# An audio tower kernel: the 3x3 convolution as four products side by side, and a new order of the pipeline behind it

## The reference, cut to what matters

```
h = signature(x) @ W.T + b                      # 64 x 63 tokens, 128 features
a = layernorm(h)
q = batchnorm(a @ Wq + bq); k = softmax(a @ Wk + bk); v = batchnorm(a @ Wv + bv)
lam_c = einsum('bukt,buvt->bkv', k, v);   Yc = einsum('bhkt,bkv->bhvt', q, lam_c)
lam_p = relu(conv3x3(v, Wpos));           Yp = einsum('bhkt,bkvt->bhvt', q, lam_p)
h = h + (Yc + Yp) @ Wout + bout
c = layernorm(h)
h = h + top1_expert(c; gate_w, w1, w2, w3) + gelu(c @ sw1.T) @ sw2.T
```

## Time and profile before

| what | value |
|---|---|
| median of 3 runs | 637.65 us |
| the profiled execution, its time | 638.09 us |
| its span, first to last instruction | 636.1 us |
| busy: PE / DVE / POOL / ACT | 587.9 / 501.1 / 304.1 / 278.7 us |
| granted TensorE clock, mean | 0.975 of full speed |

### The profile page before, as it was taken

How to read it: one execution, slowest core, us unless ns; L and a number is a source line. 1 busy time by engine, 2 the same in 40 slices (tenths; PEclk the granted TensorE clock), 3 DMA queues, 4 the chain that set the end, 5 groups by cost and what they waited for, 6 DMA issues and landing times. The chain is left out here.

```text
span 636.1 us, 13527 instructions
## 1 busy us (share of the span) xinstructions
PE 587.9 (92%) x3737; PEld 469.5 (74%) x3737; DVE 501.1 (79%) x1407; ACT 278.7 (44%) x693; POOL 304.1 (48%) x307
## 2 busy tenths in 40 slices
PE   2789999999999999999895999999999899999993
PEld 0467888888888888888663677777777678888882
DVE  6968889999999988887764788988788677777772
ACT  3332233333333332331224667676767745555541
POOL 3924334555544443320033468887767553333332
PEclk9798999999999999999998899999999999999997
DMA  8402455566665544555655545554441322222210
GB/s 285 45 1 86 153 180 179 187 196 201 202 188 184 163 145 154 163 168 169 154 125 168 126 102 135 126 130 103 112 106 46 93 77 80 74 59 76 60 32 1
DMA packets 127171, 80.02 MB, mean 126 GB/s; under 512 B 66548, under 2 KB 121485, under 8 KB 127126
## 3 DMA queue, kind: packets, MB, share of 16 engines
q1 hardware_dynamic: 122642, 72.89, 40.7%
q0 software_dynamic: 3296, 6.27, 3.1%
q10 hardware_dynamic: 1188, 0.30, 0.2%
HBM read 30.64 MB, written 49.33 MB: 126 GB/s over the span
## 5 line engine op out<-in xcount | busy, mean ns | idle before, releaser
L1251 DVE SCALAR_TENSOR_TENSOR P<-PS,QN 128x512 f32<-128x512 f32 x128 | 79.5, 683 | 26.3 <-PE PS L1430 25.7
L553 DVE SCALAR_TENSOR_TENSOR Z<-PS,Vt,Z 126x128 f32<-126x128 f32 x224 | 78.6, 351 | 8.6 <-PE PS L681 0.6
L681 PE MATMUL PS<-Wh,Ah 128*126 128x512 f32 x256 | 79.6, 434 | 0.0
L339 POOL TENSOR_TENSOR INCl<-INC,INCh 126x512 fp32r<-126x512 f32 x31 | 40.1, 1293 | 76.4 <-ACT INCh L416 76.4
L681 PE MATMUL PS<-Wl,Ah 128*126 128x512 f32 x256 | 71.9, 404 | 2.9 <-DVE Wl L517 2.9
L793 POOL DMA_INDIRECT out_h<-LC,KVH x39 | 38.0, 973 | 73.4 <-DVE LC L837 72.8
L681 PE MATMUL PS<-Wh,Al 128*126 128x512 f32 x256 | 70.7, 397 | 0.0
L681 PEld LDWEIGHTS PS<-Wl,Ah 128*126 128x126 f32 x256 | 48.8, 191 | 15.7 <-issue 3.3
L855 PE MATMUL PS<-W1h,IM 128*128 x156 | 58.7, 416 | 1.0 <-issue 1.0
L681 PEld LDWEIGHTS PS<-Wh,Al 128*126 128x126 f32 x256 | 48.3, 189 | 12.6
L456 ACT ACTIVATE XT<-PS 128x126 f32<-128x126 f32 x32 | 8.9, 277 | 108.0 <-PE PS L729 108.0
(11 more groups left out here) (230 smaller groups left out, 1480.3 us busy)
## 6 DMA issues: line engine op xcount, KB each, us to landing
routed<-nobody SPq DMA_DIRECT2D x30, 1170.0 KB, 5.3
IM<-v_pad SPq DMA_DIRECT2D x124, 72.0 KB
KVH<-routed SPq DMA_DIRECT2D x39, 130.0 KB, 2.2
WRW<-in_w SPq DMA_DIRECT2D x16, 256.0 KB, 3.1
R<-h_rows SPq DMA_DIRECT2D x16, 129.9 KB
W1l<-in_wsig SPq DMA_DIRECT2D x4, 512.0 KB, 8.8
WR<-in_w SPq DMA_DIRECT2D x8, 256.0 KB, 3.2
q_raw<-QS SPq DMA_DIRECT2D x32, 63.0 KB
```

What stands on the lines that cost most here:

```text
L339: pool.tensor_tensor(INCl[:], INC[:], INCh[:].bitcast(f32), ALU.subtract).then_inc(incl_ready, 1)
L553: ins = dve.scalar_tensor_tensor(Z[:, u], psU[h][:, d], sc, Z[:, u], ALU.mult, ALU.add)
L681: ins = pe.matmul(out, a, w, start=(n == 0), stop=(n == len(turn) - 1))
L1251: ins = dve.scalar_tensor_tensor(P[:, b, HV * h:HV * h + HV], psC[2 * pair + hb], 0.0, QN[:, g % 2, b:b + 1].broadcast_to([128, HV, SP]), ...
```

## The change

Five things change, all in `middle`.

1. `IM` holds each group's 18 rows once: at partitions 0, 32, 64 and 96 lie the 18 rows of (sequence u, channel half h), for two pairs q of sequences. `conv(g, q)` is now eight products of 18 rows and 512 columns: four with the rounded taps `WPh`, one on each row quarter, into four PSUM banks, then four with the rest `WPl`, summed into the same banks. There are 2 calls for a group, and 8 loads as before, each of half the bytes. `IM` has 3 buffers.
2. The PSUM banks are taken in pairs (`PSC`), so that `products` is one instruction of 1024 elements for a sequence, 4 for a group instead of 8 of 512.
3. `add_products` sums all 16 channels of one pair of sequences: 16 products of 128 columns, instead of 8 of 256.
4. `up` of group f = k-2 moves from the end of PE's step k-1 to the start of step k, in two halves; `down` is cut in three pieces that stand between other work.
5. POOL does `QN` of group k+1 first in its step, then `LC` of group k, then `Gl`; the low half of `W2` moves one step later. ACT copies `LS` first. SP stores chunk 1 of v before it loads `IM` of group 1, and loads `IM` of group 2 before it stores the other chunks. ACT's queue loads the raw queries of groups 1 and 2. SP loads `IM` three groups ahead.

```diff
-        def load_im(eng, g, cs=range(2)):
-            for pair in range(2):
-                for c in cs:
-                    for hb in range(2):
-                        src = v_pad[g * GB + 2 * hb + pair]
-                        eng.dma_start(IM[64 * hb + 18 * c:64 * hb + 18 * c + 18, g % 2, pair].bitcast(f32),
-                                      bass.AP(src.tensor, src.offset, [[SP, 18], [6 * SP, DK], [1, SP]])).then_inc(im_in[g % 2][pair], 16)
+        def load_im(eng, g, qs=range(2)):
+            for q in qs:
+                for u in range(2):
+                    src = v_pad[g * GB + 2 * q + u]
+                    for h in range(2):
+                        r = 32 * (2 * u + h)
+                        eng.dma_start(IM[r:r + 18, g % IB, q].bitcast(f32),
+                                      bass.AP(src.tensor, src.offset + 6 * SP * HV * h, [[SP, 18], [6 * SP, HV], [1, SP]])).then_inc(im_in[g % IB][q], 16)
@@ SP @@
             load_im(sp, 0, (0,))
-            for pair in range(2):
-                sp.wait_ge(im_in[0][pair], 64)
+            sp.wait_ge(v_ready, 4)
+            for q in range(2):
+                sp.wait_ge(im_in[0][q], 64)
+            store_v(1, v1_stored)
             load_im(sp, 1)
             load_h(0)
-            sp.wait_ge(v_ready, 4)
-            for q in range(1, 4):
-                store_v(q)
+            sp.wait_ge(v1_stored, 16)
+            load_im(sp, 2)
+            for q in (2, 3):
+                store_v(q, v_stored)
+            load_w2(0)
             load_h(1)
-            load_w2(0)
             sp.wait_ge(v_ready, 6)
             for q in range(4, G8):
-                store_v(q)
+                store_v(q, v_stored)
             load_w2(1)
-            sp.wait_ge(v_stored, 16 * (G8 - 1))
             for k in range(NG):
                 if on(k + 2, QB, NG):
                     wait_from_one(sp, qn_ready, k)
-                    load_q(k + 2)
-                if on(k + 2, 0, NG):
-                    sp.wait_ge(conv_done, 4 * k + 4)
-                    load_im(sp, k + 2)
+                    load_q(sp, k + 2)
+                if on(k + IB, 0, NG):
+                    sp.wait_ge(conv_done, 2 * k + 2)
+                    if k == 1:
+                        sp.wait_ge(v_stored, 16 * (G8 - 2))
+                    load_im(sp, k + IB)
@@ DVE @@
-                for hb in range(2):
-                    b = 2 * hb + pair
-                    ins = dve.scalar_tensor_tensor(P[:, b, HV * h:HV * h + HV], psC[2 * pair + hb], 0.0,
-                                                   QN[:, g % 2, b:b + 1].broadcast_to([128, HV, SP]), ALU.max, ALU.mult)
+                for u in range(2):
+                    b = 2 * q + u
+                    dve.scalar_tensor_tensor(P[:, b], psC[u], 0.0, QN[:, g % 2, b:b + 1].broadcast_to([128, DK, SP]),
+                                             ALU.max, ALU.mult).then_inc(p_ready, 1)
@@ PE @@
-                for hb in range(2):
-                    r = 64 * hb
-                    ins = pe.matmul(PS[2 * pair + hb][:, :], W36[r:r + 36], IM[r:r + 36, g % 2, pair, HALF * h:HALF * h + HALF],
-                                    start=True, stop=True)
+                for n, w in enumerate((WPh, WPl)):
+                    for u in range(4):
+                        rows = slice(32 * u, 32 * u + 18)
+                        ins = pe.matmul(PS[u][:, :], w[rows], IM[rows, g % IB, q], start=(n == 0), stop=(n == 1))
@@ ACT @@
+            for g in range(1, QB):
+                load_q(act, g)
```

271 lines of the change are left out of this document (133 added, 138 removed).

## The result

The changed kernel takes 643.42 us (median of 6 runs, 640.34 to 644.71), the kernel before 637.56 us in the same comparison (635.88 to 639.41). The ratio is 1.0088, 95% interval 1.0061 to 1.0115: slower by 0.9%, where 634.4 us and a gain were forecast, and outside the range.

What follows compares the result with a forecast made beforehand. PE was taken as the bound, almost full at 10.50 us a step, with a new 10.05 us loop over ACT, DVE and PE replacing it. Terms -1.0, -5.8 and +3.4 made -3.4 us: 634.4 against 637.65, range 624 to 642.

Steps and rivals of the forecast that it cites:

- The steady loop: Loop over ACT, DVE and PE sets each middle step at 10.05 us instead of 10.50: -5.8 us over 13 steps.
- PE's list: PE's own work per middle step, forecast at 9.9 us, just under the 10.05 us loop over ACT, DVE and PE.
- The weight loop: Steps 4 to 9: SP's weight, query load, POOL's QN to W2 make 10.67 us a turn; +3.4 us in all.
- the same queue, slower than before: Rival, chance 0.16: longer query landings, 0.7 us in all per 0.1; gain gone from 3.9 us, 642 at 4.5.
- no change: Rival, chance 0.13: the loop over ACT, DVE and PE is really 10.5 us, so 5.8 is lost: 637.6 us.
- the ACT loop: Another name for the steady loop over ACT, DVE and PE, forecast at 10.05 us a step.
- The opening: Up to the gate of step 2: the 5.5 us IM stall becomes a 6.6 us stall on LC; -1.0 us.
- The end: Step 16 has less between head and transposes, but one `up` moved behind it: 0, within 1 us.
- Two estimates by rules: Skill-page rules: four row tiles at 3.07 times make a convolution run 0.79 us; 62 ns per matmul makes `add_products` 2.0.
- queries in time: Rival, chance 0.20: the weight loop never binds, 631 us; with QN of group 3 also in time, 622.
- Quarters one after another: Rival, chance 0.05: the convolution's row quarters do not run side by side, PE's list is 12.3 us; about 660.
- `add_products` bound by issue: Rival, chance 0.01: `add_products` takes 2.0 us each, PE's list 11.9 us a step; about 655 us.

Runs made afterwards that it cites:

- e16: Changed kernel with four query buffers instead of three and the last part of the expert choice moved into the next step, chip E: 631.42 us, ratio 0.9919.
- e2: Changed kernel with SP's expert weight load moved one step later, behind the load of the raw queries: 639.50 us, ratio 1.0024.
- e3: Changed kernel with four raw-query buffers instead of three, loads one step earlier, and chunk 1's store sharing a semaphore: 633.59 us, ratio 0.9969.
- e5: Changed kernel with 6 more idle-filling products ahead of the first convolution and 7 more between first and second: 652.52 us, ratio 1.0221.
- e4: Kernel before with only the new store order: chunk 1 stored first, IM of group 2 loaded ahead of the other chunks: 633.82 us, ratio 0.9959.
- e10: Same program as e16 (changed kernel, four query buffers, split expert choice), on chip C, which shows late signals: 642.25 us, ratio 1.0046.

## Why the prediction was wrong

**The steady loop, 10.05 us a step and -5.8.** This is the step that failed. The mechanism was right: with the queries in time this loop sets the step. Its size was wrong, and so was what I left out of it.

| part of a turn | forecast | e16, steps 3 to 10 |
|---|---|---|
| `up` to gelu, and the two gelus | 2.08 | 2.09 |
| table load to square root | 1.40 | 1.40 |
| square root to `products`, through the normed rows | 1.24 | 1.49 |
| `products`, and waking PE | 2.42 | 2.40 |
| convolution | 0.66 | 0.67 |
| `lam` and the first half of `up` | 1.25 | 1.33 |
| `add_products` | 1.0 | 1.01 |
| sum | 10.05 | 10.39 |

The largest miss is in the normed rows. The change put GpSimd's low half of `W2` (1.29 us) beside them, and the second row instruction starts only when the low half has ended, within 0.02 us in all eight turns that have one. My 1.24 came from a step of before, where the shorter `QN` (0.73 us) stood beside them. In steps 11 to 14, where no low half is left, the same stretch takes 1.03 to 1.22 us and a turn 9.94 to 10.47. That the low half holds the rows is read from these coincidences; no run moved it.

What I left out is VectorE's expert choice. In every second step it delays the statistics, and the turn takes 10.6 to 10.8 us there (e2, e3). With the queries in time and `choose` as it was (e3) the 13 steps took 136.03 us, 0.4 less than before; with `choose` split as well (e16) 134.20, 2.3 less. The forecast was 5.8 less.

PE's list was put at 9.9 with `rank` averaged in, and is 9.9 without it and 10.3 with it, so 10.1. The 0.2 less for the convolution came (1.34 for 1.52), the 0.1 for a shape change did not, and `rank` is 0.36 in every second step for 0.3. The list did not bind, but it leaves only 0.10 in every second turn.

**The weight loop, 10.67 us and +3.4.** The mechanism was right, the size was not. The landings behind a weight took 3.8 to 4.2 us, 3.96 in the mean, for 3.4; with that my sum gives 11.23, and a turn took 11.3 in the mean. The loop cost 4 us (e2, e3) over a steady loop that was longer than thought too. My 3.4 came from the loads of before as a whole. One turn, 11.9 us, also has the lower clock in it (granted 0.57 from 386 to 390 us), and its step took 12.9.

The rival "the same queue, slower than before" came true: by its own rule, 0.7 us for each 0.1 of landing, 3.96 gives 638.3. So did, for the most part, the rival "no change": the ACT loop is 10.4 in one step and 10.6 to 10.8 in the next. I had weighed them one by one. Together, by the prediction's own terms, they make -1.0 at the opening and five steps of 0.73 more: 640.3 us, near the 640.6 of the profiled execution.

**The opening, -1.0.** Measured -0.7, with the issue of the queries at 343.66 (344.9 forecast), `QN` at 347.68 and `yc` at 350.25 (351.1). But the idle time had moved: 5 to 7 us ahead of `yc` were forecast, 0.88 came, and the rest was spent at the lower clock because the changed kernel leaves 2.4 us idle near 324 to 327. With the gap filled (e5) the wait is 5.36. Two limits one behind the other, and either alone gives nearly the same gate: the queries alone 46.09 us (e5), the clock alone 47.14 (e3), both 45.37. That the forecast of -1.0 came out is in part luck.

**The end, 0.** It became 1.6 us longer, in step 16 (9.21 for 8.48) and behind it (132.84 for 131.94); the kernels with the changed order show 141.9 to 143.9 on chips without late signals, before and e4 140.4 to 140.6. In step 16 TensorE waits 1.4 us for `Gl` before `down`, for 0.7 before. Which instruction's move costs it was not tried.

**Two estimates by rules.** Eight products of four row quarters took 0.66 us, as long as two sets of two did before. "TensorE: Matmul & The Clock Gate" of the Trainium skill, section "Measured speedup vs the span model", gives 3.07 times for four row tiles; my estimate by it was 0.79. That estimate did not come true, but it stood on my 0.22 for a set, where the sets follow each other 0.33 apart, so it does not test the page's factor. The 62 ns per matmul of the section "Wait — 56ns, not 53.3ns?", which holds where the sequencer decodes in software, would make `add_products` 2.0 us. The trace does not agree: it took 1.01, 32 ns each.

The rival "queries in time" was wrong as a forecast (631 or 622 us): e3, which puts them in time and changes nothing else, takes 633.59, with 0.4 of the 5.8 us gained in the steps. That e16 takes 631.42 is a coincidence, since it splits `choose` too. Quarters one after another and `add_products` bound by issue are ruled out by the rows above.

## What to carry to other kernels

When a loop over several engines is added up from rows of the old kernel, ask for each term what the new order puts beside it and ahead of it, and do so for every kind of step, the one with the extra work in it too. Here the normed rows got a GpSimd instruction beside them (0.25 us a step) and the statistics the expert choice ahead of them (0.2 to 0.4 in every second step), and of 5.8 us 0.4 were left. When two steps take turns in length, count them from another mark before explaining the difference. Take a load's landing from the loads that have the same neighbour ahead in the queue. When a wait is removed at the head of a pipeline, ask which wait stands behind it and whether the short gaps left will cost the clock.

## What the runs showed of the hardware

- Short idle times of TensorE can cost more than a long one, and not in every execution. e10 and e16 are one program. In e10 it idled 0.70 us for `IM` and 1.46 for `products`, in e16 1.07 and 1.46; the granted clock from 325 to 345 us was 0.84 in the one and 0.56 in the other, and the gate of step 2 came 39.92 or 47.14 us after the middle's first product. In e16 the granted clock was 0.50 from 327.5 to 354.8 us; in the kernel before, behind an idle time of 5.47 us, from 344.6 to 354.7. First e10, then e16:

```profile
325.00:345.00 20.00, 16.82 (x208) 12.23 (x208) 13.43 (x19) 7.08 (x17) 9.51 (x10) 0.84 0.63 153
```

```profile
325.00:345.00 20.00, 17.25 (x156) 12.44 (x160) 10.14 (x17) 5.55 (x11) 5.24 (x6) 0.56 0.55 144
```

  The spread of these kernels' times goes with it: of the twelve executions of e16 the two long ones (637.65 and 638.27 us) have mean granted clocks of 0.963 and 0.961, the other ten (629.8 to 633.82) 0.973 to 0.985.
- VectorE's operations on 126 by 32 elements took 0.19 or 0.75 us. The long ones lie beside GpSimd: L1266 (467.29 to 468.04) ends with GpSimd's `QN` (467.26 to 467.98), L1269 (468.51 to 469.25) with its `LC` (468.07 to 469.20). "SBUF — State Buffer" of the Trainium skill, section "Who interferes with whom", states that a VectorE instruction with two inputs in SBUF is blocked by a GpSimd instruction that reads SBUF. The trace agrees. The normed rows, two `tensor_scalar` operations (L1356 in e16), took 0.83 to 1.06 us beside the low half of `W2` and 0.60 to 0.71 where GpSimd ran only scatters; in the changed kernel, beside `Gl` and the low half, up to 1.77.
- On two of five chips TensorE's signals come up to 2.3 us late in steps 10 to 15, until 0.5 to 0.8 us behind GpSimd's second scatter. On these chips the same program took 4.5 us (changed) and 6.6 us (e10 for e16) more in steps 9 to 15 and 4 to 5 more behind them, and before 2 more in all. The cause is open.
